# One product across the chunks in place of two, placed behind the first own product; an own signal for the normed rows; another order of the drain

## The reference, cut to what matters

```python
h = attention(emb[tokens] * sqrt(d) + pos)                # a softmax over the queries
x = layernorm(h);  u = layernorm(x) * ln_w + ln_b
z, xBC, dt = split(u @ in_proj_w.T)                       # 512, 768 and 8 columns
xs, Bm, Cm = split(silu(conv4(xBC) + conv_b)); dt = softplus(dt + dt_bias)
# state space part, per sequence, chunks c = 0, 1 of 128 tokens, a = dt * A, a_cs = cumsum(a) in the chunk
Y_diag = einsum('bcln,bcsn,bhcls,bcshp->bclhp', Cc, Bc, exp(segsum(a)), xs * dt)
states = einsum('bcln,bhcl,bclhp->bchpn', Bc, exp(a_cs[-1] - a_cs), xs * dt)
Y_off  = einsum('bcln,bchpn,bhcl->bclhp', Cc, states_before, exp(a_cs))
Y = Y_diag + Y_off + D * xs
h = h + (rmsnorm(Y * silu(z)) * norm_w) @ out_proj_w.T + x
h = h + experts(layernorm(h))                             # top 2 of 8 experts, 1024 slots each
```

## Time and profile before

| | |
|---|---|
| median of 3 executions | 925.45 us (925.26 to 925.67) |
| the profiled execution's own time | 926.9 us |
| its span, first to last instruction | 925.2 us |
| PE busy | 904.3 us (98%) |
| DVE busy | 633.4 us (68%) |
| ACT busy | 528.6 us (57%) |
| POOL busy | 503.8 us (54%) |
| mean granted clock of TensorE | 0.996 |

### The profile page before, as it was taken

One profiled execution on the slowest core, in us unless ns is written; L12 is line 12 of the kernel. 1 busy time (PEld: TensorE's weight loads), 2 busy tenths in 40 slices (PEclk: granted clock), 3 DMA queues, 4 the chain that ended last, 5 costly groups with the idle time before them and its releaser, 6 DMA issues. The chain is left out here.

```text
span 925.2 us, 17776 instructions
## 1 busy us (share of the span) xinstructions
PE 904.3 (98%) x5832; PEld 806.5 (87%) x5832; DVE 633.4 (68%) x1698; ACT 528.6 (57%) x1097; POOL 503.8 (54%) x498
## 2 busy tenths in 40 slices
PE   8999999999999999999999979999999999999998
PEld 7888798888888888888888779999999999999997
DVE  1587889888988898889889644646464646464633
ACT  1767776677667766776667434444443434343533
POOL 5656877887778777876775522223232323232343
PEclk9999999999999999999999989999999999999999
DMA  7940011001000000000000044343434342523221
GB/s 211 321 154 17 30 47 34 23 34 34 13 23 14 24 13 23 14 25 12 12 14 5 25 138 122 70 109 74 108 70 112 67 115 63 119 58 79 23 58 46
DMA packets 49398, 59.13 MB, mean 64 GB/s; under 512 B 6304, under 2 KB 44683, under 8 KB 49360
## 3 DMA queue, kind: packets, MB, share of 16 engines
q1 hardware_dynamic: 35920, 42.14, 14.1%
q0 software_dynamic: 13440, 16.50, 10.7%
HBM read 33.62 MB, written 30.67 MB: 69 GB/s over the span
## 5 line engine op out<-in xcount | busy, mean ns | idle before, releaser
L690 POOL DMA_INDIRECT out<-ye,tok_slot x56 | 96.0, 1713 | 250.0 <-DMA out<-ye,tok_slot 128.0
L973 ACT ACTIVATE hf<-bank 128x512 f32<-128x512 f32 x128 | 79.3, 620 | 187.1 <-PE bank L1814 187.0
L1423 DVE TENSOR_TENSOR h_lo<-hf,h_hi 128x512 fp32r<-128x512 f32 x128 | 88.8, 694 | 101.5 <-ACT h_hi L975 100.1
L1812 PE MATMUL bank<-w_hi,h_hi 128*128 128x256 f32 x512 | 146.1, 285 | 0.0
L1813 PE MATMUL bank<-w_lo,h_hi 128*128 128x256 f32 x512 | 144.9, 283 | 0.0
L1814 PE MATMUL bank<-w_hi,h_lo 128*128 128x256 f32 x512 | 144.9, 283 | 0.0
L1122 DVE SCALAR_TENSOR_TENSOR xc<-bank,cw,xc 128x253 f32<-128x253 f32 (+2 forms) x288 | 128.2, 469 | 1.9 <-ACT xc L799 0.4
L1812 PE MATMUL bank<-xe_hi,w_hi 128*128 128x512 f32 x256 | 100.0, 391 | 0.0
L1813 PE MATMUL bank<-xe_lo,w_hi 128*128 128x512 f32 x256 | 99.8, 390 | 0.0
L1814 PE MATMUL bank<-xe_hi,w_lo 128*128 128x512 f32 x256 | 99.7, 389 | 0.0
L1813 PEld LDWEIGHTS bank<-w_lo,h_hi 128*128 128x128 f32 x512 | 98.3, 192 | 0.0
(11 more groups left out here) (223 smaller groups left out, 2352.3 us busy)
## 6 DMA issues: line engine op xcount, KB each, us to landing
w_raw<-w SPq DMA_DIRECT2D x16, 1024.0 KB
slots_dram<-zero_row SPq DMA_DIRECT2D x1, 8320.0 KB, 29.9
xe<-slots_dram SPq DMA_DIRECT2D x15, 520.0 KB, 4.5
out<-hb SPq DMA_DIRECT2D x16, 256.0 KB, 2.1
w_raw<-in_wT SPq DMA_DIRECT2D x2, 644.0 KB, 6.2
out<-zero_row SPq DMA_DIRECT2D x1, 1024.0 KB, 32.1
slots_dram<-rows,slot POOLq DMA_INDIRECT x64
out<-ye,tok_slot POOLq DMA_INDIRECT x64
```

Of the source, the lines that this page charges most:

```text
L690: g.indirect_dma_start(out, bass.IndirectOffsetOnAxis(ap=tok_slot[q][:, j:j + 1], axis=0), ye[q][:, j, :], None, compute_op=ALU.add).then_ ...
L973: sc.activation(hf[m % 2][:, :], h_bank[i % H_BANKS][:, :], ACT.Gelu_apprx_tanh)\
L1423: vc.tensor_tensor(h_lo[:, m, :], hf[m % 2][:, :], h_hi[:, m, :].bitcast(F32), ALU.subtract)\
L1812: te.matmul(out_, hi, rhi, start=first_, stop=False)
```

## The change

In every half turn with a back:

- `state_inputs` forms Bm of chunk 0 times Cm of chunk 1 (128x128) where it transposed Bm, and ACT copies it to `across`. `chunk_state`, ACT's `state` and `from_state` are gone; `across_chunks` is one 128x512 product of `across` and `xdec`, and it stands behind the first own product, in front of `to_hT`. Its result goes to bank 3.
- `normed` waits for a new semaphore `hn_coef` that `shift` raises; `residuals` now waits for `hu_coef`.
- POOL's `skip_x` waits for `decay_scores` of chunk 1.
- On DVE `times_dt` 1 stands in front of `router_in`, and `carried_y` in front of `first_y`. On PE `to_yT` 0 stands behind `project_dt`, not in front of it.

In the drain: `D * xs` is added by PE (`skips`: products of the convolution's output with `skip_diag`, diagonal matrices made once on POOL, accumulated with the own products); `decayed_x` is on ACT; DVE does the residual of batch t first, and a shorter `last_y`; most `keep_clock` are gone and `project_rows` is in two parts around `to_yT` 1; `to_v2T` of t goes in front of them. In the last half turn `choices_before` of the other batch goes first, and the last batch's `describe_rows` is on DVE, so POOL has only the scatter left. In the final half turn with a front POOL's `gated_root` goes in front of `segment_inputs`. Before the experts `keep_clock` is 3 for 6.

```diff
-            DRAIN = dict(rows=2, seg0=1, seg2=8, state=2, out=2)
-            LAST = dict(v2T=10, route=2, choices=9)
+            DRAIN = dict(rows=2)
+            LAST = dict(first=9, v2T=2, route=2, choices=9)
 # POOL norm_roots
-                g.tensor_tensor(shift..., lnr..., lnm..., ALU.mult)
+                g.tensor_tensor(shift..., lnr..., lnm..., ALU.mult).then_inc(hn_coef[p], 1)
 # POOL half, with a front
                 if b:
+                    pool.wait_ge(m_ready[KD - 1][q], m_ready[KD - 1].now(b, q))
                     skip_x(b, q, 0)
                     skip_x(b, q, 1)
+                if b and not t:
+                    skip_matrices()
 ...
                 if not nf:
+                    gated_root(b, q)
                     segment_inputs(f, p, 0)
-                    gated_root(b, q)
 # ACT normed, residuals, half
-                act.wait_ge(hu_coef[p], hu_coef.now(r, p))
+                act.wait_ge(hn_coef[p], hn_coef.now(r, p))
...
                 if f:
                     normed(f, p)
-                if b:
-                    state(b, q)
                 if f:
                     mixer_input(f, p)
 # ACT, in the drain only
+            def decayed_x(r, p):
+                ...
+                for h in range(NH):
+                    at = slice(h * HD, (h + 1) * HD)
+                    ins = sc.activation(xdec[p][:, at], xdt[p][:, 0, at], ACT.Copy, scale=edec[p][:, h:h + 1])
 # DVE half, with a front
+                if b:
+                    times_dt(b, q, 1)
                 if t:
                     router_in(t, p)
-                if b:
-                    times_dt(b, q, 1)
                 if b:
                     decay_scores(b, q, 1)
                 if t:
                     router_top(t, p)
                 if b:
+                    carried_y(b, q, bank[q][3])
                     first_y(b, q)
-                    carried_y(b, q)
 # DVE, drain
+                    residual(t, p, p)
                     mask_scores(b, q, p)
                     segment_inputs(b, q, seg_hi, a_hi)
-                    times_dt(b, q, 0)
+                    times_dt_early(b, q, 0)
                     segment_inputs(b, q, seg_lo, a_lo)
-                    times_dt_early(b, q)
                     decay_scores(b, q, 0)
+                    times_dt_early(b, q, 1)
                     decay_scores(b, q, 1)
-                    residual_sum(t, p, p)
-                    first_y(b, q)
-                    carried_y(b, q)
-                    second_y(b, q)
-                    residual_norm(t, p)
+                    last_y(b, q)
                     mean_square(b, q)
-                    residual(b, q, p)
+                    residual_sum(b, q, p)
                     router_in(t, p)
+                    residual_norm(b, q)
 # PE
-                    te.transpose(bank[where][3][:, 0:P], xc[p][:, KI, 0:P], ident[:, :])
+                    te.matmul(bank[where][3][:, 0:P], xc[p][:, KI, 0:P], xc[p][:, KI + 1, P:2 * P], start=True, stop=True)
...
-                te.matmul(bank[p][3][:, :], bs[p][:, :], xdec[p][:, :], start=True, stop=True)\
-                    .then_inc(state_psum[p], 1)
+                te.matmul(dst[:, :], across[p][:, :], xdec[p][:, :], start=True, stop=True)\
+                    .then_inc(yo_psum[p], 1)
...
                 if b:
                     segment_sums(b, q, 3)
-                    chunk_state(b, q)
                     own_chunk(b, q, 0)
+                    across_chunks(b, q, bank[q][3])
...
                 if f:
                     to_hT(f, p)
-                if b:
-                    from_state(b, q)
                 if b:
                     own_chunk(b, q, 1)
                 if t:
                     choices_before(t, p)
-                if b:
-                    to_yT(b, q, 0)
...
                     project_dt(f, p)
+                if b:
+                    to_yT(b, q, 0)
+                if f:
                     project_channels(f, p, 0)
...
-                    keep_clock(0, 6)
+                    keep_clock(0, 3)
```

More of the change, by code:

```diff
@@ L237, in lm_block @@
         gm = pair("gm", [P, KD, P])
[L238 removed]
+        across = pair("across", [P, P])
+        skip_diag = fb("skip_diag", [P, KI, P])
         xdec = pair("xdec", [P, DI])
[L240 removed]
         h2 = pair("h2", [P, KD, DM])
@@ L637, in half @@
                     if b:
[L638 to L641, removed]
+                        second_root(t, p)
+                        pool.wait_ge(y_ready[q], y_ready.now(b, q, 1))
                         with_bias(Turn(b.reg, b.shift - 1), q)
-                        second_root(t, p)
                         gated_root(b, q)
@@ L843, in x_rows @@
                 copy(xs[p][:, c, :], bank[p][XS_BANK[c]][:, :], xs_ready[p])
-            def state(r, p):
-                act.wait_ge(state_psum[p], state_psum.now(r, p))
-                copy(st[p][:, :], bank[p][3][:, :], st_ready[p])
             def square(r, p, c):
@@ L1193, in second_y, with last_y @@
                     own = back.mark(vc.tensor_tensor(y[p][:, 1, :], bank[p][YD_BANK[1]][:, :], y[p][:, 1, :], ALU.add))
+                    gated(r, p, 1, own)
+                def last_y(r, p):
+                    dve.wait_ge(yd_psum[p], yd_psum.now(r, p, 1))
+                    dve.wait_ge(sz_ready[p], sz_ready.now(r, p))
+                    vc.tensor_tensor(y[p][:, 0, :], bank[p][YD_BANK[0]][:, :], sz[p][:, 0, :], ALU.mult)\
+                        .then_inc(y_ready[p], 1)
+                    carried_y(r, p, bank[1 - p][1])
+                    back.wait(carried_y.last)
+                    dve.wait_ge(yd_psum[p], yd_psum.now(r, p))
+                    own = back.mark(vc.tensor_tensor(y[p][:, 1, :], bank[1 - p][3][:, :], y[p][:, 1, :], ALU.add))
                     gated(r, p, 1, own)
@@ L1339, in half @@
                     dt_in(f, p)
+                if not f:
+                    describe_rows(t, p)
                 if t:
@@ L1645, in own_chunk, with skips, own_on_skips @@
                     ins.then_inc(yd_psum[p], 1)
-                def from_state(r, p):
-                    pe.wait_ge(st_ready[p], st_ready.now(r, p))
-                    pe.wait_ge(decay_ready[p], decay_ready.now(r, p))
-                    te.matmul(bank[p][2][:, :], xc[p][:, KI + 1, P:2 * P], st[p][:, :], start=True, stop=True)\
-                        .then_inc(yo_psum[p], 1)
+                def skips(r, p, c):
+                    if c == 0:
+                        pe.wait_ge(decay_ready[p], decay_ready.now(r, p, 1))
+                    else:
+                        pe.wait_ge(s_diag, 1)
+                        pe.wait_ge(bs_ready[p], bs_ready.now(r, p))
+                        pe.wait_ge(gm_ready[p], gm_ready.now(r, p))
+                    for m in range(KI):
+                        te.matmul((bank[p][YD_BANK[0]], bank[1 - p][3])[c][:, m * P:(m + 1) * P], xc[p][:, m, c * P:(c + 1) * P],
+                                  skip_diag[:, m, :], start=(m == 0), stop=False)
+                def own_on_skips(r, p, c):
+                    pe.wait_ge(m_ready[c][p], m_ready[c].now(r, p))
+                    pe.wait_ge(xdt_ready[p], xdt_ready.now(r, p, c + 1))
+                    for h in range(NH):
+                        ins = te.matmul((bank[p][YD_BANK[0]], bank[1 - p][3])[c][:, h * HD:(h + 1) * HD], seg[p][:, c, h, :],
+                                        xdt[p][:, c, h * HD:(h + 1) * HD], start=False, stop=(h == NH - 1))
+                    ins.then_inc(yd_psum[p], 1)
                 def to_yT(r, p, c):
```

90 lines of the change are left out of this document (50 added, 40 removed).

## The result

The changed kernel takes 932.42 us (median of 6, 928.40 to 937.77), the kernel before 925.53 us in the same job (924.86 to 926.41): ratio 1.0074, 95% interval 1.0055 to 1.0092, slower by 0.7%. The forecast was 926.0 with a range up to 930; the time lies outside it. The profiled execution took 933.68 us.

The account below looks back on a forecast made before the run. It took the chain of DVE and ACT to bound the changed loop: +3.6 there, -0.3 and +0.1 beside it, -2.4 drain, -0.4 before the experts, +0.6 us in sum; 926.0 us on the median, range 914 to 930.

Parts of the forecast that it names:

- PE's saving becomes idle time on PE: Loop: PE's 0.75 us saved per half turn turns into idle time on PE, since DVE's chain sets the pace.
- DVE's chain: Loop, nmax to next nmax: five links sum to 31.32 us per half turn against 31.04, +3.6 us over 13.
- hn's own signal: Loop: normed stops waiting for hu_s, ending PE's 0.48 us of idle in every second half turn.
- The skips' wait: Loop, POOL and DVE: lock passes from seg to oh; seg to y takes 3.55 us, where 3.32 and 3.49 stood.
- Rival A: Loop: skips miss router_top, oh is not held, the chain is 30.42 us; about 914.5 us in all; chance 27%.
- Rival B: Loop: PE is the bound and DVE's chain gives way, 29.73 us a half turn; 905 us; chance 5%.
- Rival C: Drain: residual at the head of DVE's list delays later work 1.4 us with nothing given back; 929 us; chance 23%.
- Rival D: Loop: hn still starts late because seg holds shift; time near the forecast's; shares the forecast's 45% chance.
- The drain and the experts' start: After the loop: drain -2.4 us from earlier last scatters, and -0.4 us before the experts from fewer instructions.
- the last scatters: Drain, POOL: the last four start at about 532.6 us for 534.98, with no wait between the two scatter groups.
- Up to the first of the 13 half turns: First half turn with a back, 33.8 to 64.9 us, without a routing batch: -0.3 us.

Follow-up runs that it names:

- fill_clock: Changed kernel plus four throwaway identity products per half turn on PE: one ahead of own_chunk 0, two ahead of project_dt, one ahead of to_yT 0; 926.68 us.
- fill_dt: Changed kernel plus two throwaway products per half turn on PE, between choices_before and project_dt; 926.99 us.
- b_short1: Kernel before, with from_state computing only 64 of its 512 columns, order and waits unchanged; 922.15 us.
- b_short2: Kernel before, with from_state and chunk_state each computing only 64 of 512 columns; 954.76 us.
- router_first: Changed kernel with times_dt 1 put back behind router_in on DVE; 961.79 us.
- bias_later: Changed kernel with POOL's with_bias moved behind second_root; 940.90 us.
- skips_early: Changed kernel without skip_x's new wait for decay_scores of chunk 1; 927.73 us.
- across_first: Changed kernel with the product across the chunks ahead of own_chunk 0 in the loop; 935.28 us.
- loop_b_drain_a: Half turns of the kernel before with hn's own signal, plus the changed kernel's drain and start of the experts; 919.49 us, 0.9928 of the kernel before.
- yT_first: Changed kernel with to_yT 0 put back ahead of project_dt on PE; 948.95 us.

## Why the prediction was wrong

**The step that failed** is "PE's saving becomes idle time on PE", costed at nothing. It became idle time, and in it the granted clock fell to 0.50, which cost 4.7 us in the loop and about 2.3 in the last half turn, 7.0 us; 926.0 and 7.0 is 933, the median was 932.4. I had read the clock as 0.996 and gone on, and no rival had a price for it. PE had stood nowhere between two groups of 8-column products then, and the change made such a place: it takes `from_state` away and moves `to_yT` 0 from between `choices_before` and `project_dt` to behind them.

`fill_clock` and `fill_dt` show that PE's idle time brings the falls: with products in the gap they go. `b_short1` shows that its amount alone does not decide, `b_short2` and `router_first` that more of it makes it worse. That the place between 8-column products matters more than others is supported and not shown. For it: five falls with 0.28 us there, one with 0.49 us ahead of 128-column transposes. Against its being the only one: the fall at 493 us, six of the 12 in `bias_later` and many in `router_first` begin 17 us into the half turn, behind a wait ahead of `own_chunk` 0. A gap of the same length, moved within one kernel, and a filler where PE does not wait, were not tried.

**DVE's chain**: right. 31.29 us without falls for 31.32, and +3.2 us for the +3.6 forecast. In the half turn shown the first four links came out within 0.04, the fifth 0.16 longer. The idle time of PE was not 1.6 us a half turn as I had it but 0.46: the view counts a product as busy to its modelled end, and fillers worth 0.88 us fit into a gap of 0.46 without making the half turn longer.

**hn's own signal**: right, and on its own worth 3 us, which the rest of the change's loop gave away again.

**The skips' wait**: right in kind, its cost about 0.2 us a half turn. `oh` takes 0.98 us beside a skip. The Trainium skill (SBUF — State Buffer, section Who interferes with whom) has a port pair locked for a whole instruction; the trace agrees: `oh` ends at 274.05 us, with the second skip (274.00), and takes 0.19 to 0.20 us in the half turns of `skips_early`, where the skips come earlier, so it is held and not merely slowed. Rival A, that `oh` is missed, is excluded.

**Rival B** (PE the bound) is excluded by 31.3 where its floor was 29.7, and by fillers of 0.88 us that left it at 31.3. **Rival C** put a slower result in the drain; the drain gave its gain. **Rival D** did not occur.

**The drain and the experts' start**: -3.7 for -2.8; the last scatters gained 3.0 for 2.4, though POOL did wait 0.88 us between the two groups, which I had excluded. Up to the first of the 13 half turns it was +0.3 us for the -0.3 I took. The misses of the chain, the drain and this (-0.4, -0.9 and +0.6) come to -0.7, which brings the 933 above to the 932.4 measured. In the chances, rival C enters the sum for slower with 0.22, not with its 0.23.

What stays open: why a gap of 0.28 us brings a fall in five of the 13 half turns and not in each (those of 190.73, 316.99 and 443.71 us have one at the same place, those between mostly none), and why `across_first` with the same gap has more of them. The Trainium skill (TensorE: Matmul & The Clock Gate, section A second HAM failure mode: psum-queue depth-cycling) tells of another kernel, with 512-column bf16 products, in which frequent short idle times between groups of products made the clock swing; the runs here agree, with gaps of 0.28 to 1.41 us, and suggest that the products around the gap matter too.

## What to carry to other kernels

Time taken from TensorE is not free where another engine sets the pace: ask where the idle time will lie, and if it comes between products of few columns, look at the granted clock in windows of 1 us, not at the page's tenths alone. Leave in the product that covers such a gap, or fill it: two throwaway products of 0.22 us were worth 5 us here. And ask of a move that makes one instruction early what it will then collide with: `with_bias` moved gained 0.9 us at nmax and lost 0.75 at the next product on DVE. When a change has several parts, time them one by one: here the hn signal (-3) and the drain (-3.7) were both good and hidden by the part between them.

## What the hardware showed that I had not expected

- Behind a gap of 0.28 us between 8-column products, with PE otherwise busy by the view, the granted clock went to 0.50 for 3.4 us in five of 13 half turns. The half turns with a fall take 31.9 to 33.0 us for 31.3, and one without a fall behind them 30.67, so a fall costs 0.9 us on the mean (4.7 us for five).
- A gap of 0.49 us before 128-column transposes, in 14 of 16 half turns of `b_short1`, brought one fall in the loop.
- The spread of times grows with the falls: 919.13 to 919.92 us in `loop_b_drain_a`, which has none in its half turns, 928.40 to 937.77 in the changed kernel, 939.39 to 954.82 in `yT_first`. Here a wide spread was itself a sign of the clock.
